# A conditioned transformer kernel on one core: reordered first embedding round, wide scale-and-shift matmuls, later GpSimd masks, gate steps moved between W1 and W2

## What is computed

```
L0: h = gelu(x @ down_W.T + down_b); h = h @ expert_W[id].T + expert_b[id] (if id is valid) + domain_emb[id]
    x = layernorm(h @ up_W.T + up_b + x) * gamma + beta
L1: scale, shift = split(silu(sin_emb(timestep)) @ W_ada + b_ada)
    x = ln(x) * (1 + scale) + shift; q, k, v = x @ Wq + bq, x @ Wk + bk, x @ Wv + bv      (16 heads of 32)
    p = softmax(where(mask, -inf, q @ k.T / sqrt(32) + bias)); x = x + (p @ v) @ Wo + bo
    x = x + gelu2((ln(x) * g2 + beta2) @ W1 + b1) @ W2 + b2
L2: pairs of columns rotated by theta and phi
L3: U, V = gram_schmidt(U), gram_schmidt(V)              (32 columns each); basis = U @ V.T
    gate = sigmoid(relu(mean_s(x) @ gate_w1.T + gate_b1) @ gate_w2.T + gate_b2) * sigmoid(safety)
    out = x + gate * ((x @ basis) @ basis.T[:, :32] @ resp_w.T + resp_b + safety_bias)
```

## Time and profile before

| | us |
|---|---|
| three runs, median (lowest, highest) | 3651.71 (3650.6, 3653.76) |
| the profiled execution, its own time | 3659.26 |
| its span, first to last instruction | 3657.1 |
| TensorE busy | 3576.4 (98%) |
| embedding, attention, rest (from the stretches below and the last row of the span) | 0 to 511.9, to 2552.8, to 3657.1 |

### The profile page before, as it was taken

The page is one execution under the profiler, slowest core; times in us unless marked ns, Lnnn a source line. Parts: engine busy times, 40 slices in busy tenths (PEclk is TensorE's granted clock), DMA queues, the critical chain, the costliest instruction groups (busy, mean ns, idle before and its releaser), DMA issues. The chain is left out here.

```text
span 3657.1 us, 79807 instructions
## 1 busy us (share of the span) xinstructions
PE 3576.4 (98%) x32028; PEld 2465.6 (67%) x32028; DVE 2269.9 (62%) x4509; ACT 2184.4 (60%) x3040; POOL 2059.0 (56%) x778
## 2 busy tenths in 40 slices
PE   5999989999999999999999999999999999999999
PEld 3444458888888888888888888888444444444444
DVE  5766758888888888888888888887211111111102
ACT  2433449999999999999999999998110210110110
POOL 1111149899998989899989899996310110110100
PEclk7999999999999999999999999999999999999998
DMA  4455489888898888988888988887300110110002
GB/s 158 184 194 198 172 340 355 319 320 325 339 374 333 323 328 325 370 344 324 323 324 335 387 329 323 325 322 258 128 23 12 35 35 12 47 46 28 30 23 92
DMA packets 211165, 828.34 MB, mean 226 GB/s; under 512 B 26208, under 2 KB 60144, under 8 KB 135536
## 3 DMA queue, kind: packets, MB, share of 16 engines
q1 hardware_dynamic: 204432, 814.83, 59.1%
q10 hardware_dynamic: 6368, 8.42, 0.6%
HBM read 731.93 MB, written 91.23 MB: 225 GB/s over the span
## 5 line engine op out<-in xcount | busy, mean ns | idle before, releaser
L1169 POOL TENSOR_TENSOR at_tiles<-at_tiles,at_negmask 128x1792 f32<-128x1792 f32 x509 | 1828.2, 3634 | 208.5 <-DMA at_tiles<-in_bias 177.3
L1259 ACT ACTIVATE at_tiles<-at_tiles,at_rmin 128x2048 f32<-128x2048 f32 x512 | 1025.2, 2002 | 54.8 <-DVE at_rmin L1306 54.1
L1205 PE MATMUL at_ps_p<-consts,at_tiles 128*128 128x128 f32 x8192 | 1026.1, 272 | 0.1
L1205 PEld LDWEIGHTS at_ps_p<-consts,at_tiles 128*128 128x128 f32 x8192 | 931.5, 142 | 36.6 <-ACT at_prob_t L1267 0.4
L1267 ACT ACTIVATE at_prob_t<-at_ps_p 128x512 f32<-128x512 f32 x1536 | 833.1, 597 | 128.5 <-PE at_ps_p L1205 126.9
L1306 DVE CUSTOM_DVE_ANT_0 at_tiles<-at_ps_s,at_tiles 128x1024 f32<-128x1024 f32 x512 | 624.4, 1219 | 116.9 <-PE at_ps_s L1186 113.0
L1186 PE MATMUL at_ps_s<-at_k_stack,at_q_stack 128*128 128x512 f32 x2048 | 676.2, 431 | 5.1 <-DVE at_rmin L1306 3.1
L1306 DVE CUSTOM_DVE_ANT_0 at_tiles<-at_ps_s,at_tiles,at_rmin 128x1024 f32<-128x1024 f32 x512 | 657.5, 1284 | 18.6 <-PE at_ps_s L1192 0.3
L1222 PE MATMUL at_ps_c<-at_prob_t,at_v 128*32 128x128 f32 x16384 | 500.3, 274 | 0.6 <-DVE at_ctx_rows L1324 0.6
L1222 PEld LDWEIGHTS at_ps_c<-at_prob_t,at_v 128*32 128x32 f32 x16384 | 431.6, 110 | 43.8 <-issue 43.0
L1553 PE MATMUL ff_ps_m<-ff_norm_t,ff_w 128*128 128x512 f32 x1024 | 445.4, 595 | 0.5 <-ACT ff_feats L1692 0.5
(11 more groups left out here) (187 smaller groups left out, 2634.0 us busy)
## 6 DMA issues: line engine op xcount, KB each, us to landing
at_tiles<-in_bias SPq DMA_DIRECT2D x512, 1024.0 KB, 7.0
at_k_stack<-k_hi SPq DMA_DIRECT2D x128, 256.0 KB, 5.2
at_k_stack<-k_lo SPq DMA_DIRECT2D x128, 256.0 KB, 5.2
negm<-em_mask_out SPq DMA_DIRECT2D x32, 512.0 KB, 6.6
at_q_stack<-q_hi SPq DMA_DIRECT2D x128, 128.0 KB, 5.0
at_q_stack<-q_lo SPq DMA_DIRECT2D x128, 128.0 KB, 5.1
at_v<-v SPq DMA_DIRECT2D x64, 256.0 KB, 7.8
at_negmask<-negm SPq DMA_DIRECT2D x32, 512.0 KB, 9.9
```

The costliest lines, as they stand in the source:

```text
L1169: pool.tensor_tensor(tiles[s][:, 0:PCOLS], tiles[s][:, 0:PCOLS], negm[s][:, 0:PCOLS], ALU.add).then_inc(s_pool, 1)
L1205: last = pe.transpose(ps_p[k][:, y * P:(y + 1) * P], tiles[s][:, t * P:(t + 1) * P], ident)
L1259: act.activation(tiles[s][:, :], tiles[s][:, :], ACT.Exp, bias=rmin[:, s, 1:2], scale=-1.0, accum_out=rsum[:, s:s + 1]).then_inc(s_exp, 1)
```

## The change

In round 0: VectorE does the angles first, then the expert weights of batch 0; sines and silu come ahead of the gelu and of em_hid. Scale and shift are worked out by eight matmuls with the SiLU's 2 columns as the stationary and 512 columns of W_ada as the moving operand, into two rows (one per batch); bias and the 1 are added to the rows, and eight small transposes give the columns. The bias is loaded by one transfer instead of eight. Only two Gram-Schmidt steps remain in the round, the second at its very end, and on VectorE behind them stand tile 1's bias additions and the expert weights of batch 1. ScalarE takes tile 1's columns ahead of the unit rows. Rounds 6 and 7 have five steps each. GpSimd waits for all splits (s_split at 64) before its first masks. In ffn_stage the gate's matmuls come after the W1 groups 8 to 11 and after 12 to 15, ScalarE's sigmoid behind all gelus, the response of tile 0 behind the first W2 group.

```diff
@@ -131,7 +131,8 @@
...
-    STEPS = RANK // NT
+    GS_STEPS = [2] + [4] * (NT - 3) + [5] * 2
+    GS_FIRST = [sum(GS_STEPS[:n]) for n in range(NT + 1)]
@@ -169,8 +170,8 @@
...
-        ada_rows = sb("em_ada_rows", [4 * DC, P])
-        b_ada = sb("em_b_ada", [P, 2 * DC])
+        ada_rows = sb("em_ada_rows", [B, 2 * D])
+        b_ada = sb("em_b_ada", [B, 2 * D])
@@ -443,25 +442,27 @@
...
-            def ada_columns():
+            def ada_matmuls():
                 pe.wait_ge(s_wada, 16)
                 pe.wait_ge(s_silu, 1)
+                for k in range(2):
+                    for c in range(DC):
+                        last = pe.matmul(ps_q[k][0:B, :], sig[:, c * B:(c + 1) * B], w_ada[:, c, k * D:(k + 1) * D],
+                                         start=(c == 0), stop=(c == DC - 1))
+                    last.then_inc(s_adt, 1)
+
+            def ada_columns():
+                pe.wait_ge(s_adrc, 2)
                 for o in range(2 * DC):
-                    for c in range(DC):
-                        last = pe.matmul(ps_q[0][:, o * B:(o + 1) * B], w_ada[:, c, o * P:(o + 1) * P],
-                                         sig[:, c * B:(c + 1) * B], start=(c == 0), stop=(c == DC - 1))
-                last.then_inc(s_adt, 1)
-
-            def ada_to_rows():
-                pe.wait_ge(s_adc, 1)
-                pe.transpose(ps_q[1][0:4 * DC, 0:P], ada_col[:], ident).then_inc(s_adr, 1)
+                    last = pe.transpose(ps_q[2][:, o * B:(o + 1) * B], ada_rows[:, o * P:(o + 1) * P], ident[0:B, 0:B])
+                last.then_inc(s_adr, 1)
 
@@ -508,10 +509,10 @@
...
                 if r == 0:
-                    ada_columns()
+                    ada_matmuls()
...
-                if front:
+                if 1 <= r < NT:
                     gs_dots(r, 1)
@@ -523,11 +524,13 @@
...
                 if back:
                     project(p, 6)
+                if 1 <= r < NT and GS_STEPS[r] == 5:
+                    gs_dots(r, 2)
...
                 if back:
                     project(p, 7)
-                if front:
+                if 1 <= r < NT and GS_STEPS[r] == 4:
                     gs_dots(r, 2)
@@ -537,18 +540,22 @@
...
                     x_columns(r + 1, (2, 3))
-                if front:
+                if r == 0:
+                    ada_columns()
+                if 1 <= r < NT:
                     gs_dots(r, 3)
-                if r == 0:
-                    ada_to_rows()
                 if back:
                     project(p, 10)
+                if 1 <= r < NT and GS_STEPS[r] == 5:
+                    gs_dots(r, 4)
...
                 if front:
                     x1_columns(r, (2, 3))
+                if r == 0:
+                    gs_dots(0, 1)
@@ -559,9 +566,7 @@
...
-            for c in range(2 * DC):
-                part = given["b_ada"][c * P:(c + 1) * P].rearrange("(p a) -> p a", a=1)
-                act.dma_start(b_ada[:, c:c + 1], part).then_inc(s_bada, 16)
+            act.dma_start(b_ada[:], rows(given["b_ada"], B)).then_inc(s_bada, 16)
@@ -610,6 +615,7 @@
...
             take_x(0, range(DC))
+            sines()
             for r in range(NT + 1):
@@ -617,8 +623,6 @@
...
-                if r == 0:
-                    sines()
                 if back:
@@ -629,12 +633,14 @@
...
                 if back:
                     take_qk(p, 7)
+                if r == 0:
+                    take_x(1, range(DC))
                 if front:
...
-                if r + 1 < NT:
+                if 1 <= r < NT - 1:
                     take_x(r + 1, range(DC))
@@ -661,12 +667,14 @@
...
             for r in range(NT):
-                gs_norms(r, 0)
+                if r >= 1:
+                    gs_norms(r, 0)
                 root(r, 0)
-                gs_norms(r, 1)
+                gs_norms(r, 0 if r == 0 else 1)
                 root(r, 1)
-                gs_norms(r, 2)
-                gs_norms(r, 3)
+                for k in range(1 if r == 0 else 2, GS_STEPS[r]):
+                    gs_norms(r, k)
+            pool.wait_ge(s_split, 8 * NT)
@@ -783,6 +791,9 @@
...
             def angles():
 
+                dve.wait_ge(s_const, 16)
+                dve.wait_ge(s_int, 4 * 16)
+                link(v.tensor_copy(idf[:], ints[:]))
                 link(v.tensor_scalar(idf[:, 0, :], idf[:, 0, :], 1.0 / 100.0, 4000.0, ALU.mult, ALU.mult))
@@ -835,20 +843,21 @@
...
-            def take_ada():
-                dve.wait_ge(s_adt, 1)
-                dve.wait_ge(s_bada, 2 * DC * 16)
-                by_kind = ada_col[:].rearrange("p (b k c) -> p k c b", b=B, k=2)
-                bias_of = b_ada[:].rearrange("p (k c) -> p k c", k=2)
+            def take_ada_rows():
+                dve.wait_ge(s_bada, 16)
                 for k in range(2):
-                    link(v.tensor_tensor(by_kind[:, k], ps_q[0][:, k * DC * B:(k + 1) * DC * B].rearrange("p (c b) -> p c b", b=B),
-                                         bias_of[:, k, :].unsqueeze(2).broadcast_to([P, DC, B]), ALU.add))
-                scales = ada_col[:].rearrange("p (b k c) -> p b k c", b=B, k=2)[:, :, 0, :]
-                v.tensor_scalar(scales, scales, 1.0, None, ALU.add).then_inc(s_adc, 1)
-
-            def take_ada_rows():
+                    part = slice(k * D, (k + 1) * D)
+                    dve.wait_ge(s_adt, k + 1)
+                    v.tensor_tensor(ada_rows[:, part], ps_q[k][0:B, :], b_ada[:, part], ALU.add).then_inc(s_adrb, 1)
+                dve.wait_ge(s_adrb, 1)
+                v.tensor_scalar(ada_rows[:, 0:D], ada_rows[:, 0:D], 1.0, None, ALU.add).then_inc(s_adrc, 1)
+                dve.wait_ge(s_adrb, 2)
+                v.nop().then_inc(s_adrc, 1)
+
+            def take_ada_columns():
                 dve.wait_ge(s_adr, 1)
-                v.tensor_copy(ada_rows[:], ps_q[1][0:4 * DC, 0:P]).then_inc(s_adrc, 1)
+                v.tensor_copy(ada_col[:].rearrange("p (b k c) -> p k c b", b=B, k=2),
+                              ps_q[2][:, 0:2 * DC * B].rearrange("p (k c b) -> p k c b", k=2, c=DC)).then_inc(s_adc, 1)
 
@@ -862,14 +871,15 @@
...
+            angles()
             expert_weights(0)
-            angles()
...
             dve.wait_ge(s_gsw, 2 * 16)
             gs_products(gs[0], first)
+            silu()
             for r in range(NT + 1):
@@ -882,24 +892,26 @@
...
+                if 1 <= r < NT:
+                    gs_squares(r, 0)
                 if front:
-                    gs_squares(r, 0)
                     residual(r, 0)
...
+                if 1 <= r < NT:
+                    gs_project(r, 0)
                 if front:
-                    gs_project(r, 0)
                     residual(r, 2)
...
+                if r == 0:
+                    gs_squares(0, 0)
                 if back:
                     split(p, 2)
-                if r == 0:
-                    silu()
                 if not front:
@@ -908,8 +920,9 @@
...
+                if 1 <= r < NT:
+                    gs_squares(r, 1)
                 if front:
-                    gs_squares(r, 1)
                     centred(r, 2)
@@ -918,14 +931,17 @@
...
+                if 1 <= r < NT:
+                    gs_project(r, 1)
                 if front:
-                    gs_project(r, 1)
                     row_stats(r, 1, 1)
...
+                if r == 0:
+                    take_ada_rows()
                 if back:
@@ -933,36 +949,50 @@
...
                 if r == 0:
-                    take_ada()
+                    take_ada_columns()
+                    gs_project(0, 0)
+                    gs_squares(0, 1)
+                    gs_project(0, 1)
+                    add_up_bias(1, range(TJ))
+                    expert_weights(1)
                 if back:
                     split(p, 6)
+                five = 1 <= r < NT and GS_STEPS[r] == 5
+                four = 1 <= r < NT and GS_STEPS[r] == 4
                 if not front:
                     take_end(4)
                     v.tensor_copy(net.ident_bf[:], ident)
                     rotation_rows()
+                if five:
+                    gs_squares(r, 2)
                 if back:
                     split(p, 7)
-                if front:
+                if five:
+                    gs_project(r, 2)
+                if four:
                     gs_squares(r, 2)
                 if back:
                     take_v(p, 0)
-                if front:
+                if four:
                     gs_project(r, 2)
                 if back:
                     take_v(p, 1)
-                if front:
+                if four or five:
                     gs_squares(r, 3)
-                if r + 1 < NT:
+                if 1 <= r < NT - 1:
                     add_up_bias(r + 1, range(TJ))
+                if five:
+                    gs_project(r, 3)
                 if back:
                     take_v(p, 2)
-                if front:
+                if four:
                     gs_project(r, 3)
```

(23 more changed lines are left out.)

25 lines of the change are left out of this document (10 added, 15 removed).

## The result

The changed kernel took **3627.67 us** (median of 4 runs, 3625.14 to 3630.03); the kernel before, beside it, 3651.51 (4 runs, 3650.60 to 3653.76). Ratio 0.9934, 95% interval 0.9916 to 0.9951: faster, by 24 us or 0.7%. Its profiled execution took 3630.03 with a span of 3627.9; against the profiled 3659.26 of before that is 29.2 less. The forecast was 3621 for the median, in a range of 3612 to 3634, and 3628.3 for the profiled execution.

A forecast was written before the change was run, and what follows sets the result against it. It took time to lie where TensorE idles or runs at half clock. Terms -20.5 + 3.0 - 8.8 - 5.5 = -31.8, taken as 31, gave 3628.3 us for the profiled execution and 3621 for the median, range 3612 to 3634.

The forecast's parts named there:

- Round 0: Start of the kernel: an earlier em_hid, no idle 13.07 us and fewer Gram-Schmidt steps bring tile 1's down projection forward; minus 20.5.
- a clock "that may not be back at once": End of round 0: 1.0 us given back in that round's sum for TensorE's clock returning late.
- Rounds 6 and 7: A fifth Gram-Schmidt step in each brings TensorE stalls and two more dots: plus 3.0, bounds 0.5 and 6.
- Masks: Last round: with GpSimd's first masks behind the splits, TensorE's idle time and half clock go; minus 8.8.
- gate: Feed-forward: later gate matmuls remove 3.58 us of idle time and 1.7 of slow clock; minus 5.5, bounds 4.5 and 6.
- rival C: Masks or late steps cost more: V takes held, stalls at their upper bound, 3 + 3, giving 3627; chance 0.08.
- A: Round 0: the wide scale-and-shift matmuls run at 1.2 GHz; plus 5, giving 3626; chance 0.13.
- B: End of round 0: transposes do not restore the clock, down projection and first Q group at 1.2 GHz; plus 4, 3625; chance 0.07.
- D: Start of the kernel: first loads land earlier, the chain from 11.11 starts up to 4 us earlier; 3617; chance 0.08.
- E: Attention: its loads fall worse against TensorE, 0.08 us a unit, plus 41, giving 3662, slower than before; chance 0.01.
- F: Round 0 is bound by a load, such as tile 1's x, and its first part is lost: 3636; chance 0.04.
- take the same difference off the median: Whole kernel: the sum made against the profiled 3659.26 is also subtracted from the median 3651.7, giving 3621.

The follow-up runs named there:

- after_again: The changed kernel unchanged, run once more beside the kernel before on the same chip: 3625.53 us, ratio 0.9919 against the kernel before.
- one_step: bias_dots_later with Gram-Schmidt steps dealt 1, 4, 4, 4, 4, 5, 5, 5, so one step leaves round 0 and round 5 gets a fifth: 3621.37 us.
- bias_dots_later: Changed kernel with round 6's bias additions behind step 3's projection, and step 4's dots in rounds 6 and 7 behind half of x1's columns: 3625.79 us.
- before_again: The kernel before unchanged, run once more for a second profile and its spread: 3657.48 us, ratio 1.0001.
- masks_gate: The kernel before with GpSimd's wait ahead of its first masks and the gate edits, round 0 and steps as before: 3643.69 us, ratio 0.9966.
- masks_alone: The kernel before with one change, GpSimd waiting for the 64 split pieces ahead of its first masks: 3652.95 us, ratio 0.9985.
- gate_alone: The kernel before with only the edits of the first gate and the response: 3651.63 us, ratio 0.9981.
- narrow_first: The changed kernel with the former 64 two-column scale-and-shift records added, unused, ahead of the wide matmuls: 3634.52 us, ratio 0.9939.
- narrow_again: The changed kernel with the former 64 two-column records, their bias transfers and row layout in place of the wide matmuls: 3630.04 us, ratio 0.9930.

## Why the prediction was right, and where it was off

**Round 0: right in total (-20.68 by -20.5) and nearly step by step.** Em_hid 24.89 (24.7), unit rows 44.96 (44.3), the 2x512 row work 1.64 (1.8), wide matmuls 7.03 at full clock (7.0), down projection of tile 1 at 54.14 (53.9), em_hid of tile 1 at 64.95 (66.3) and so no stall there (1.0 forecast). The clock took 1.59 where 1.0 stood, which with 0.2 less in the down projection's start made up for it; in the second pair of profiles the clock took 3.1 and the whole round gave 18.48. So that the total agreed to 0.2 is in part luck. The forecast allowed for a clock "that may not be back at once" without saying what takes it. It was the 3.53 in which TensorE waits for VectorE, the cover that the prediction counted as free. The step that the sum took as one block, wide matmuls and reordering, is now divided in two: 2.4 to 4.5 for the shape, the rest for the order.

**Rounds 6 and 7: the term was mis-sized, +5.45 by +3.0, inside its bounds of 0.5 and 6.** The 2.0 us stall was there as 1.81. The wait for the dots of step 2 in round 6 (0.48) was taken up by ScalarE's, as counted: that one shrank by 0.76, from 1.19 to 0.43. What the step left out is the clock behind the stall, 1.73, and a wait of 0.29 ahead of the down projection of round 7. A wait also costs about 0.26 more than its length, as what runs on into the next group otherwise (0.16) and a slower first record (0.1) come on top, net four times. Together: 0.48 + 1.81 + 0.29 - 0.76 + 1.73 in round 6, 0.49 + 1.01 - 1.0 in round 7, four times 0.26 and two dots of 0.17 are 5.43. In after_again, where the clock held, the term is 3.75. These 2.4 are also why the attention started 23.9 us earlier and not 26.

**Masks (-8.62 by -8.8) and gate (-5.56 by -5.5): right**, each alone and both together. The V takes beside the masks were not held (0.69), so rival C's first half falls; its second nearly came, with +5.45 of its bound of 6. At the gate the half microsecond counted for the gate's own matmuls was 0.11 (0.92 to 0.81 between the starts); the rest of the 5.56 is the 3.58 of idle time, 1.69 of clock and the run-on.

**The rivals.** A fell, and its price was measured at 3.9 instead of 5. B was half there: after 0.50 through all the transposes at the end of round 0 the clock was not back at the down projection, for 1.6 and 3.1 us in the two profiles, but it was in the first Q group. In one_step and bias_dots_later it came back within the transposes and dots there, at 52 to 54, so neither B nor its opposite is a rule. D fell: the integers landed at 10.43 to 11.29 in the eight profiles with one bias transfer and at 10.40 to 11.75 in the six with eight, and as the two overlap, no gain is shown. E: the attention took 1.45 more in one pair of profiles and 0.46 in the other, within its spread over the profiles here (2044.3 to 2046.6, by the marks of the table). F did not come.

**The step that failed is the first paragraph's: "take the same difference off the median".** The sum for the profiled execution was 3628.3 and it took 3630.03. For the median it gave 3621, and 3627.67 and 3625.53 were measured; the change was worth 24 where 31 stood. The median of the three runs shown (3651.71) was not what the kernel before usually takes: in 53 later runs it lay between 3649.6 and 3661.5, 44 of them above 3654, around 3658, like both its profiles (3659.26, 3658.07). The profile was the typical run and the three were low, as was the fourth that joined them in the comparison; why all four were is not known. By two pairs of profiles the change is worth 29.2 and 29.4, 2 less than the sum, by the medians of before_again and after_again 31.9. The interval of that comparison (0.9906 to 0.9933) goes from 24 to 34 us, so that it meets the 31 so closely is luck.

**What stays open.** Why the kernel before spreads over 12 us and the changed one over 5. With both waits gone (masks_gate) five runs lie within 1.2 us, and masks_alone and gate_alone spread over 6.8 and 3.0. So the spread seems to go with the waits of the last round and the gate, though five runs are few. It does go with the clock: the mean granted clock listed with each of the 53 runs is 0.988 or 0.989 in eight of the nine below 3654 and 0.985 to 0.987 in 43 of the 44 above. In which stage the low ones kept it is not shown, as no profile of one was caught; before_again, taken for that, has 3658.07. That masks_alone gained 5.3 by the medians and 8.8 by the profiles may have the same cause.

## What to carry to other kernels

Set a sum made from a profile against that profile, and take the kernel's usual time from many runs: three runs can all lie at one end. Price a wait on TensorE as its length and a range for the clock behind it (0 or 1.7 us for the wait of 1.8 in round 6). Where matmuls run slow, look up by stretches when the clock fell: in round 0 it had fallen over 8 us ahead of the wait that seemed to blame. And look for the work that can be queued between the waiting matmul and what it waits for. In a queue written by hand, moving a late consumer one position can take away a whole wait at no cost that shows, as bias_dots_later does.

## What was not expected of the hardware

Unbroken TensorE work can lose the granted clock: with the 64 records of 32 fp32 matmuls of two moving columns it fell from 1.00 to 0.50 while TensorE was never idle (narrow_first, narrow_again), and the same products with 512 moving columns and two stationary ones held it (after) or regained it (behind the narrow ones). A record of two moving columns takes 0.11 us from start to start at full clock and 0.21 at half. Additions of 2x512 out of PSUM take 0.62 us each where two follow one another (1.24) and 0.65 to 0.68 alone, those of 128x512 0.64 (two in 1.27) and 0.69: two partitions are as slow as 128. A clock that was down came back late or early behind the same work: in the same stretch of transposes and dots it was back at 52 to 54 in one_step and bias_dots_later, and only at 57 and 60, within the down projection, in the two profiles of the changed kernel.
